# Routing in PSUM, later early moments, and a reordered start in an attention and mixture-of-experts kernel

## The reference

```python
x = x + attn(layernorm(x))          # attn returns h + z, h its input
x = x + ffn(layernorm(x))           # the same, x + y is returned

# attn, h = layernorm(x)
q, k, v = h @ w_q, h @ w_k, h @ w_v               # for each head
z = softmax(q @ k.T / 8) @ v                      # for each head
return h + concat(z) @ w_o

# ffn, t = 4096 tokens, cap = 512 tokens for each of 8 experts
probs = softmax(xf @ Wr); eidx = argmax(probs); p_tok = probs[eidx]
rank = number of earlier tokens with the same eidx
keep = rank < cap
y[token] = p_tok * (relu(xf[token] @ W1[e]) @ W2[e])    # kept tokens only
```

## Time and profile before

| | us |
|---|---|
| median of 3 runs (1584.79 to 1588.75) | 1586.42 |
| profiled execution | 1590.52 |
| its span, first to last instruction | 1588.8 |

### The profile page before, as it was taken

The page is one execution under the profiler, slowest core; times in us unless marked ns, Lnnn a source line. Parts: engine busy times, 40 slices in busy tenths (PEclk is TensorE's granted clock), DMA queues, the critical chain, the costliest instruction groups (busy, mean ns, idle before and its releaser), DMA issues.

```text
span 1588.8 us, 21747 instructions
## 1 busy us (share of the span) xinstructions
PE 1499.3 (94%) x7396; PEld 868.9 (55%) x7396; DVE 1079.7 (68%) x1319; ACT 817.1 (51%) x1597; POOL 1192.9 (75%) x679
## 2 busy tenths in 40 slices
PE   4999999999999999999999999999998989998295
PEld 2555555555555555555555555555565556554175
DVE  6577766677666777666776667777777786774232
ACT  2556555555555555555555555555654546453221
POOL 1798877787877878787777778788777978787324
PEclk8999999999999999999999999999999999999598
DMA  4333343433233333323322333333331333314230
GB/s 115 80 82 84 96 107 91 110 87 69 63 71 81 84 83 84 83 68 84 71 63 62 74 82 84 84 84 81 70 76 36 98 84 95 77 36 118 88 114 32
DMA packets 114510, 128.38 MB, mean 81 GB/s; under 512 B 40490, under 2 KB 65583, under 8 KB 114400
## 3 DMA queue, kind: packets, MB, share of 16 engines
q1 hardware_dynamic: 107488, 116.62, 30.9%
q0 software_dynamic: 2560, 6.14, 1.1%
q10 hardware_dynamic: 4352, 4.23, 0.8%
HBM read 18.91 MB, written 12.65 MB: 20 GB/s over the span
## 4 chain that ended last, share of the span: by engine, by line
PE 87%; DVE 5%; POOL 4%; issue 1%; DMA 1%; ACT 1%; another core or an unknown queue 0%; SPq 0%; POOLq 0%; DVEq 0%; ACTq 0%
PE ps_w L1089 26%; PE ps_w L1075 16%; PE ps_w L1076 14%; PE ps_m L1033 10%; PE ps_m L1107 3%; PE ps_m L1015 3%; PE ps_w L1099 3%; POOL acc L482 3%; PE ps_m L1006 2%; PE ps_m L1007 2%; PE ps_m L1008 2%; DVE mxw L842 2%; PE ps_w L1286 1%; POOL tokens_by_slot L457 1%; PE ps_m L1286 1%
## 5 line engine op out<-in xcount | busy, mean ns | idle before, releaser
L482 POOL TENSOR_TENSOR acc<-acc,ring 128x1024 f32<-128x1024 f32 x382 | 907.5, 2376 | 160.2 <-ACT ring L627 118.1
L842 DVE TENSOR_REDUCE mxw<-ps_m 128x1 f32<-128x1024 f32 x508 | 598.1, 1219 | 345.9 <-PE ps_m L1033 341.2
L627 ACT ACTIVATE ring<-ps_w 128x512 f32<-128x512 f32 x1024 | 544.7, 597 | 125.1 <-PE ps_w L1076 121.1
L1089 PE MATMUL ps_w<-ring,V 128*64 128x512 f32 x2048 | 467.7, 598 | 0.0
L1075 PE MATMUL ps_w<-queriesA,keysA 128*128 128x512 f32 x1024 | 433.7, 423 | 0.4 <-ACT ring L627 0.4
L1076 PE MATMUL ps_w<-queriesB,keysB 65*128 65x512 f32 x1024 | 408.4, 399 | 0.0
L1089 PEld LDWEIGHTS ps_w<-ring,V 128*64 128x64 f32 x2048 | 135.7, 136 | 265.6 <-issue 227.1
L482 POOL TENSOR_TENSOR acc<-ring 128x1024 f32<-128x1024 f32 x64 | 153.1, 2393 | 133.4 <-ACT ring L627 133.3
L1075 PEld LDWEIGHTS ps_w<-queriesA,keysA 128*128 128x128 f32 x1024 | 195.6, 191 | 89.4 <-issue 45.8
L851 DVE RECIPROCAL sums<-sums 128x128 f32<-128x128 f32 x252 | 229.0, 930 | 10.6 <-ACT sums L618 10.6
L1076 PEld LDWEIGHTS ps_w<-queriesB,keysB 65*128 65x128 f32 x1024 | 195.9, 191 | 34.7 <-issue 0.8
(11 more groups left out here) (140 smaller groups left out, 976.7 us busy)
## 6 DMA issues: line engine op xcount, KB each, us to landing
queriesA<-qk_high SPq DMA_DIRECT2D x248, 128.0 KB
keysB<-qk_high SPq DMA_DIRECT2D x124, 128.0 KB
keysA<-qk_rest SPq DMA_DIRECT2D x124, 128.0 KB, 2.4
queriesB<-qk_rest SPq DMA_DIRECT2D x124, 128.0 KB, 2.4
keysA<-qk_high SPq DMA_DIRECT2D x93, 128.0 KB
tokens_by_slot<-blank ACTq DMA_DIRECT2D x16, 258.0 KB, 4.0
ring<-tokens_by_slot SPq DMA_DIRECT2D x8, 516.0 KB, 7.3
wst<-in_L_attn_w_q SPq DMA_DIRECT2D x32, 64.0 KB, 2.1
```

Source lines behind the costliest of these rows:

```text
L482: pool.tensor_tensor(acc[h][:, :], before, P_both(kt), ALU.add).then_inc(summed, 1)
L627: act.activation(P_tile(kt, p), ps_s[k % 3][:, :], ACT.Exp, scale=SCALE).then_inc(exp_done, 1)
L842: dve.tensor_reduce(mxw[h][:, p * HT + qt:p * HT + qt + 1], ps_v[banks][p], AX_X, ALU.max).then_inc(maxed, 1)
L1089: mm = pe.matmul(ps_z[p * DK:(p + 1) * DK, :], V[par][:, kt * P + p * DK:kt * P + (p + 1) * DK], P_tile(kt, p), start=(kt == 0), stop=(kt ...
```

## The change

Four things are changed.

1. **Routing.** `choose` is no longer split around the maxima and copies nothing out: all its steps read or write the bank, in three 64-column areas (`steps_of`), and the last writes the one-hot as bf16. TensorE's visit waits for its end (`onehot_ready`). `add_totals` sums the one-hot of a sequence, and `count_ranks` adds these totals by one more matmul for each earlier sequence, in place of the running counts `seen`. `find_slots` runs at once, ahead of the maxima of the visit, with rank and overflow in PSUM and two fused steps; the visit waits for its end. What doesn't need the bank (`find_shares`) comes after the maxima.
2. **Early moments** are made in parts 0 and 2.
3. **Start.** The low parts of the first keys are made by GpSimd, from a copy that ScalarE makes (`first_keys`), ahead of `residual(0)`. The turn of the first maxima comes right behind the second query projection, and `project_v` goes behind the fifth visit. `project_qk(1, 1, 1)` with its cast and remainder moves into part 0 of pair 0, beside `project_qk(1, 1, 2)`, which is given the bank `lent_turn` and comes behind the values projection.
4. TensorE runs 16 matmuls on the identity before the first transposes, and two memsets go.

The diff, cut (declarations, `ROUTED`, `part_of`, `shares`, `make_logits` and the calls at the tail follow the same pattern; `ROUTED` holds one entry a sequence):

```diff
-            return ps_s[1] if (j, use) == (1, 0) else lent_qk
+            return {(1, 0): ps_s[1], (1, 2): lent_turn}.get((j, use), lent_qk)
...
         first_q = [ps_m[1][:, 0:HALF], ps_s[0]]
+        first_keys = ring[:, 0:S]
         first_rest_k, first_rest_q = (a[:, :].bitcast(F32R) for a in acc)
...
+        def hot_of(u):
+            t = part_of(u)
+            return hot_b[:, t.start * E:t.stop * E]
...
+        def steps_of(u, bank):
+            nt = ROUTED[u][2]
+            return [bank[:, k * QT * E:(k * QT + nt) * E].rearrange("p (t e) -> p t e", e=E) for k in range(3)]
...
                     if g == 0:
-                        sp.wait_ge(first_low, 4)
+                        sp.wait_ge(first_low, 2)
+                        sp.dma_start(queriesB[0][1][0:DK, c].bitcast(F32),
+                                     first_rest_q[own[1], c].bitcast(F32)).then_inc(first_placed[g], 16)
+                        sp.wait_ge(first_key_low, 4)
                         for p in range(2):
                             sp.dma_start(keysA[0][p][own[1 - p], :].bitcast(F32),
                                          first_rest_k[own[p], :].bitcast(F32)).then_inc(first_placed[0], 16)
-                    sp.wait_ge(first_low, 6 + 2 * g)
-                    sp.dma_start(queriesB[0][1][0:DK, c].bitcast(F32),
-                                 first_rest_q[own[1], c].bitcast(F32)).then_inc(first_placed[g], 16)
-                    if g == 0:
                         place_max(0, 0, 0)
+                    else:
+                        sp.wait_ge(first_low, 4)
+                        sp.dma_start(queriesB[0][1][0:DK, c].bitcast(F32),
+                                     first_rest_q[own[1], c].bitcast(F32)).then_inc(first_placed[g], 16)
...
+            for g in range(2):
+                pool.wait_ge(first_copied, g + 1)
+                c = slice(g * HALF, (g + 1) * HALF)
+                for p, r in enumerate((slice(0, DK), slice(DK, P))):
+                    pool.tensor_tensor(first_rest_k[r, c], first_keys[r, c], keysA[0][p][r, c].bitcast(F32),
+                                       ALU.subtract).then_inc(first_key_low, 1)
+                    pool.wait_ge(first_key_low, 2 * g + p + 1)
             residual(0)
...
-                    if oct < 2 and not last:
+                    if known(j, 0) and oct == 0:
+                        cast_qk(1, 1, 1)
+                    elif oct < 2 and not last:
                         cast_qk(j + 1, nxt, 2 + oct)
...
+                    if known(j, 0) and oct == 0:
+                        cast_qk(1, 1, 2)
...
+            for g in range(2):
+                act.activation(first_keys[:, g * HALF:(g + 1) * HALF], first_k[g], ACT.Copy).then_inc(first_copied, 1)
+            copy_max(0, 0, lent_max)
             cast_first(4, first_q[1], queriesA, second_half)
             cast_qk(1, 1, 0)
             copy_v(0, 0, 0, ps_s[2])
             copy_v(0, 0, 1, ps_z)
-            copy_max(0, 0, lent_max)
-            cast_qk(1, 1, 1)
...
+            def choose(u, bank):
+                nt, t = ROUTED[u][2], part_of(u)
+                made, same, marked = steps_of(u, bank)
+                top, first_e = (cols[:, k, t] for k in range(2))
+                dve.wait_ge(logits_done, u + 1)
                 dve.wait_ge(consts, 3)
-                dve.tensor_copy(l, lent_turn[:, 0:QT * E].rearrange("p (t e) -> p t e", e=E)).then_inc(logits_copied, 1)
-                dve.wait_ge(logits_copied, b + 1)
-
...
+                then(dve.tensor_reduce(top, made, AX_X, ALU.max))
+                dve.tensor_tensor(ex[:, t, :], made, wide(top, nt), ALU.subtract).then_inc(shifted, 1)
+                then(dve.tensor_tensor(same, made, wide(top, nt), ALU.is_equal))
+                then(dve.scalar_tensor_tensor(out=marked, in0=same, scalar=-float(E), in1=iota_e[:, 0:nt, :],
+                                              op0=ALU.mult, op1=ALU.add))
+                then(dve.tensor_reduce(first_e, marked, AX_X, ALU.min))
+                dve.tensor_tensor(hot_of(u).rearrange("p (t e) -> p t e", e=E), marked, wide(first_e, nt),
+                                  ALU.is_equal).then_inc(onehot_ready, 1)
+
+            def add_totals(u):
+                dve.wait_ge(onehot_ready, u + 1)
+                with nc.allow_low_precision(reason="counts of at most eight tiles are exact"):
+                    dve.tensor_reduce(totals[:, u, :], hot_of(u).rearrange("p (t e) -> p e t", e=E), AX_X,
+                                      ALU.add).then_inc(totals_ready, 1)
+
+            def find_slots(u, bank):
+                nt, t = ROUTED[u][2], part_of(u)
+                made, kept, last_step = steps_of(u, bank)
+                rank, past = (last_step[:, :, k] for k in range(2))
+                first_e, slot = (cols[:, k, t] for k in (1, 2))
+                dve.wait_ge(ranks_done, u + 1)
+                then(dve.tensor_tensor(kept, made, hot_of(u).rearrange("p (t e) -> p t e", e=E), ALU.mult))
+                then(dve.tensor_reduce(rank, kept, AX_X, ALU.add))
                 dve.tensor_scalar(past, rank, float(CAP), float(E * CAP), ALU.is_ge, ALU.mult)
-                then(dve.tensor_scalar(slot, first_e, float(E), float(CAP), ALU.add, ALU.mult))
-                then(dve.tensor_tensor(slot, slot, rank, ALU.add))
-                dve.tensor_tensor(scatter_at[:, b * QT:(b + 1) * QT], slot, past, ALU.add)
-                dve.wait_ge(route_exp, b + 1)
-                then(dve.tensor_reduce(total, x, AX_X, ALU.add))
-                dve.reciprocal(rows[b % 2][:, :, 2 * D], total).then_inc(index_ready, 1)
+                then(dve.scalar_tensor_tensor(out=slot, in0=first_e, scalar=float(CAP), in1=rank,
+                                              op0=ALU.mult, op1=ALU.add))
+                dve.scalar_tensor_tensor(out=scatter_at[:, t], in0=past, scalar=float(E * CAP), in1=slot,
+                                         op0=ALU.add, op1=ALU.add).then_inc(ranks_read, 1)
...
+            def find_shares(u):
+                b, t0, nt = ROUTED[u]
+                total = cols[:, 3, part_of(u)]
+                dve.wait_ge(route_exp, u + 1)
+                then(dve.tensor_reduce(total, ex[:, part_of(u), :], AX_X, ALU.add))
+                dve.wait_ge(ranks_read, u + 1)
+                dve.reciprocal(rows[b % 2][:, t0:t0 + nt, 2 * D], total).then_inc(index_ready, 1)
...
+                    if first and oct == 0:
+                        low_qk(1, 1)
                     if oct < 2 and not last:
                         low_qk(j + 1, 2 + oct)
...
                     if routed(j, "c") is not None and oct == 2:
-                        choose(routed(j, "c"), 0)
+                        choose(routed(j, "c"), lent_turn)
                     if routed(j, "d") is not None and oct == 0:
-                        find_slots(routed(j, "d"), 0)
+                        find_slots(routed(j, "d"), lent_turn)
...
-                    if early(j, 1) is not None and oct < 2:
-                        first_moments(early(j, 1), oct)
+                    if early(j, 1) is not None and oct in (0, 2):
+                        first_moments(early(j, 1), oct // 2)
                     if routed(j, "a") is not None and oct in (0, 2):
                         second_moments(routed(j, "a"), oct // 2)
                     if routed(j, "c") is not None and oct == 2:
-                        choose(routed(j, "c"), 1)
-                        choose(routed(j, "c"), 2)
+                        add_totals(routed(j, "c"))
                     if routed(j, "d") is not None and oct == 0:
-                        find_slots(routed(j, "d"), 1)
+                        find_shares(routed(j, "d"))
 
             first_half, second_half = slice(0, HALF), slice(HALF, S)
-            low_first(0, first_k[0], keysA, [first_rest_k] * 2, first_half)
-            low_first(2, first_k[1], keysA, [first_rest_k] * 2, second_half)
             low_first(4, first_q[0], queriesA, [queriesB[0][0], first_rest_q], first_half)
             for v in range(4):
                 for p in (1, 0):
                     reduce_max(v, 0, v, p, 1 - v % 2)
             low_first(6, first_q[1], queriesA, [queriesB[0][0], first_rest_q], second_half)
-            for use in range(2):
-                low_qk(1, use)
+            low_qk(1, 0)
             for p in (1, 0):
                 reduce_max(4, 1, 0, p)
             in_order(dve, pair)
...
+            def spin(times):
+                for _ in range(times):
+                    pe.matmul(ps_z[:, 0:P], ident[:, :], ident[:, :], start=True, stop=True)
...
                     pe.wait_ge(first_placed[0], 16 * 7)
-                    pe.wait_ge(first_low, 8)
-                    pe.wait_ge(qk_low, 2)
+                    pe.wait_ge(first_low, 4)
+                    pe.wait_ge(qk_low, 1)
...
+            def count_ranks(u, bank):
+
+
+                nt = ROUTED[u][2]
+                made = steps_of(u, bank)[0]
```

(33 more changed lines are left out.)

92 lines of the change are left out of this document (29 added, 63 removed).

## The result

The changed kernel takes 1570.73 us (median of 5 runs, 1569.68 to 1575.4) where the kernel before takes 1588.17 (5 runs, 1584.79 to 1589.15): a ratio of 0.9902, 95% interval 0.9881 to 0.9923. Its profiled execution took 1569.68 us, 1567.9 of it the span.

The account below looks back on a forecast made before the run. TensorE was taken to bound regular pairs, so time could come only from longer pairs, the start and the tail. Terms -14.8+0.2+0.1-0.9-4.5+4.8 gave -15.1 us, from the median 1586.4 to 1571.3; range 1564 to 1579.

Parts of the forecast that it names:

- Routing steps: Pairs 26, 28 and 30: steps with an operand or result in PSUM aren't held by GpSimd's adds; -14.8 us.
- Rival 3: Pairs 26 and 28: the stall is only halved, -7 us instead of -14.8, giving 1579.1 us; chance 0.05.
- rival 4: New routing steps held too, each still having one SBUF operand; slower, about 32 us in all, 1603 us; chance 0.04.
- rival 5: Routing steps in PSUM cost the price on their page: 1.5 us more, 1572.8 us; chance 0.05.
- Choosing: Pairs 25, 27 and 29: TensorE's visit waits for the whole of `choose`; +0.2 us for the three.
- Ranks: `count_ranks` loses one matmul but takes one more for each batch before; +0.1 us.
- Tail: Serial chain of choosing and slots behind the last pair: four steps go, less two matmuls; -0.9 us.
- Start: Before pair 0: key remainders on GpSimd, maxima turned earlier, projection 1 moved into pair 0; -4.5 us, bounds -1.5 and -6.5.
- Early moments: Pairs 0 to 2: part 1 relieved, but GpSimd waits and delays TensorE and its clock; +4.8 us, bounds -1.7 and +7.

Follow-up runs that it names:

- second set: The changed kernel, not edited, run again beside the kernel before: ratio 0.9882 [0.9865, 0.9898], median 1574.14 us.
- steps_in_sbuf: The changed kernel with two of the three areas of the routing steps in SBUF, order unchanged: 0.9945 of the kernel before, 1582.57 us.
- logits_first_only: The changed kernel with only the logits moved ahead of the values projection in pairs 25, 27 and 29: 0.9885 of the kernel before, 1568.55 us.
- moments_back: The changed kernel with the early moments back in parts 0 and 1: 0.9862 of the kernel before, 1571.34 us.
- moments_only: The kernel before with nothing changed but the early moments, in parts 0 and 2: 1.0029 of the kernel before, 1597.22 us.

## Why the prediction was right

The time forecast was 1571.3 us, and 1570.7 was measured. That the two are within 0.6 us is luck in part: the forecast was a gain of 15.1 us on a median of 1586.42, and the five runs of the kernel before have 1588.17. The gain is 17.4 us by these medians, 15.6 by the ratio (12 to 19 by its interval) and 18.7 in the second set. The parts, by the prediction's steps:

- **Routing steps, -14.8.** Right in size and mechanism: 7.88, 6.65 and 0.52 us in pairs 26, 28 and 30 make 15.05. The steps run at 0.15 to 0.23 us beside the adds, and steps_in_sbuf shows the counterpart. Rival 3 (half the stall) falls, as line 1041 has no idle time left there, and rival 4 (steps in PSUM held as well) by the 0.97 us of the five steps. Rival 4's assumption of one SBUF operand was indeed met (lines 842, 845 and 847 have one), and they weren't held.
- **PSUM's own price, rival 5.** The same reduction of 64 columns takes 0.23 us with its source in PSUM (line 843) and 0.22 in SBUF (line 845 of steps_in_sbuf), and the next step starts 0.27 and 0.25 us behind its start. 0.01 to 0.02 us was the price here. The Trainium skill ("VectorE: DVE Perf Modes", "The TRN2 errata") has a fixed part of 120 cycles for a PSUM source against 58, at 0.96 GHz; the 0.065 us a step estimated from that doesn't show at these sizes, and the measurement decides.
- **Choosing, +0.2.** Too small by 0.6, and above the dear end of 0.2 a pair: the three visits wait 0.2 us each and the parts grow by 0.24 to 0.29. The chain of six steps was right, 1.41 us for the 1.44 forecast, but nothing was put in for the way from the last step's end to the visit: in pair 25 (VectorE's, then TensorE's timeline) the last step ends at 1166.12 and the visit starts at 1166.37. logits_first_only takes the 0.8 us back whole.

```profile
1165.89 0.23 DVE L827 TENSOR_TENSOR one_hot_b<-ps_m,routing_columns 128x64 bf16<-128x64 f32 x1
...
1166.37 0.73 PE L1068 MATMUL ps_m<-keysA,queriesA 64*128 64x512 f32 x4 [0.20 <-DVE one_hot_b L827]
```

- **Ranks, +0.1.** Not seen: the stretches with `count_ranks` take 10.71, 10.77 and 10.79 us where they took 10.76, 10.78 and 10.79.
- **Tail, -0.9.** From the first VectorE step on the last logits to the first scatter it is 4.30 us (1472.62 to 1476.92) where it was 5.17 (1488.29 to 1493.46): -0.87. The further 4.5 us of the tail in the first profile were luck of that execution.
- **Start, -4.5.** -5.6 in the time alone, -5.6 to -6.6 in three profiles. The working put the maxima at 18.2, the scores of pair 0 at 34.0 and the visit at 41 to 43.5; it was 16.70, 32.32 and 40.02. What was mis-sized is the stretch ahead of the maxima: the maxima were to begin 0.4 us earlier, and the matmuls ahead of everything were given 0 to 1. VectorE's timeline has the maxima 1.95 us earlier than the earlier trace rows, and GpSimd's begins the key remainders at 16.62 instead of 18.0; the four take 5.30 us, 1.3 each, as priced:

```profile
16.70 2.35 DVE L875 TENSOR_REDUCE mxw<-ps_w 128x1 f32<-128x1024 f32 x2
...
16.62 5.30 POOL L467 TENSOR_TENSOR acc<-ring,keysA 64x512 fp32r<-64x512 f32 x4 [10.60 <-ACT ring L716]
```

 Without the 16 matmuls ahead the first cast is 1.59 us later and the first value matmul 0.9 at most; with the keys on VectorE the maxima are 0.54 us later and the first value matmul 0.58. The chain of placements for pair 1 was named rightly as the next late thing. VectorE's remainder of projection 2 waits 3.07 us for one of them, and TensorE's visit 1.08 us for this remainder:

```profile
39.27 0.69 DVE L863 TENSOR_TENSOR qk_rest<-ps_m,qk_high 128x512 fp32r<-128x512 f32 x1 [3.07 <-DMA queriesB<-qk_rest]
...
40.02 0.73 PE L1068 MATMUL ps_m<-keysA,queriesA 64*128 64x512 f32 x4 [1.08 <-DVE qk_rest L863]
```

 The clock stayed at full in 32.3 to 40.6, where before it was at half from 38.5 to 41; this too I had left open.
- **Early moments, +4.8.** The mechanism came as written: GpSimd stands still (forecast 7.4 us, 7.49), the token split is late, TensorE idles in pair 1 (forecast 3.0, 3.43) and the clock is at half (forecast 2.5, 2.6; in three other profiles with this stall 1.7 to 1.8, as it was at half for 3.4 us and not 6.9). The relief of part 1 is 0.85 us in pairs 1 and 2, as forecast. The later adds of GpSimd cost 1.5 us, where I had 1.0: the softmax sums wait 0.52 us for them in one part each of pairs 2 and 3, and these parts are 0.73 and 0.75 us longer. Another 0.7 in pair 4 is a wait of 0.65 us for a placement of maxima, which the second profile of the same kernel doesn't have. In all it is +6.6 in the stretch against moments_back (6.0 in the second profile), and +4.8 in the stretch and +4.6 in the time of moments_only.

The sum is so close because errors went both ways as well: up to +1.8 in the stretch of the moments and +0.6 at choosing against -1.1 to -2.1 at the start. Moments and start are inside their bounds (the start but for 0.1 us in one profile), choosing isn't. What no part of the working held is the fall of the clock in pairs 25, 27 and 29, up to 5 us an execution; that is about the spread of the changed kernel's own runs (1569.68 to 1575.4), and which of them had it can't be told from their times.

## What to carry to other kernels

Where VectorE has small steps that someone waits for and GpSimd runs long adds in SBUF beside it, put an input of each step in PSUM: moving only the intermediate steps, with the same order and count, was worth 9.9 us over three such places here. (Whether a result in PSUM alone would do, no run shows.) When work moves to an idle place on one engine, look at who waits for its result, and follow that engine's queue on to the next consumer: an engine without slack hands on the whole delay, and here the same relief came 8 us cheaper by placing the work ahead of that waiter. Compare stretches of a trace rather than whole spans when a version's gain is as small as the noise of a tail.
